# First self attention of a decoder kernel: negative maximum copied into the score banks ahead of the products, rests and maximum on row halves of the array, heads in four steps

## The reference

```python
N_HEADS = 16; HEAD_DIM = 64; SCALE = HEAD_DIM ** (-0.5)
xq = jnp.einsum('bsh,oh->bso', x, wq)          # x: (4, 1024, 256), wq: (1024, 256)
...                                            # xk and xv in the same way
xq = xq.reshape(bsz, N_HEADS, seqlen, HEAD_DIM)   # a reshape, not a transpose
scores = softmax(jnp.einsum('bhid,bhjd->bhij', xq, xk) * SCALE, axis=-1)
out = jnp.einsum('bhij,bhjd->bhid', scores, xv).reshape(bsz, seqlen, N_HEADS * HEAD_DIM)
x = layernorm(x + jnp.einsum('bso,ho->bsh', out, wo))
```

## Time and profile before

| | |
|---|---|
| median of 3 runs | 2979.84 us (2973.99 to 2980.66) |
| profiled execution, first to last instruction (span) | 2978.0 us |
| busy, share of the span: PE | 2631.8 us, 88% |
| DVE | 1704.5 us, 57% |
| ACT | 1190.8 us, 40% |
| POOL | 1621.4 us, 54% |
| first self attention, last `take_out` (L677) | 1738.0 us from the start |

### The profile page before, as it was taken

The page is one execution under the profiler, slowest core; times in us unless marked ns, Lnnn a source line. Parts: engine busy times, 40 slices in busy tenths (PEclk is TensorE's granted clock), DMA queues, the critical chain, the costliest instruction groups (busy, mean ns, idle before and its releaser), DMA issues. The chain is left out here.

```text
span 2978.0 us, 43667 instructions
## 1 busy us (share of the span) xinstructions
PE 2631.8 (88%) x12081; PEld 1634.0 (55%) x12081; DVE 1704.5 (57%) x3436; ACT 1190.8 (40%) x1678; POOL 1621.4 (54%) x1343
## 2 busy tenths in 40 slices
PE   7999999999999999999999968982795588798695
PEld 5666666666666666666666534441574244454254
DVE  5666666656666666665666635662234555468743
ACT  3444444444444444444444324541222333454234
POOL 3666776767766677676776753424334313333343
PEclk8999999999999999999999979996897599899798
DMA  6565455555446445455544320003993100000232
GB/s 176 113 136 113 105 120 113 123 115 114 109 113 138 108 109 121 109 122 114 118 112 108 76 68 23 2 2 126 343 347 128 41 0 1 30 2 9 61 116 88
DMA packets 407010, 303.20 MB, mean 102 GB/s; under 512 B 293558, under 2 KB 338910, under 8 KB 401790
## 3 DMA queue, kind: packets, MB, share of 16 engines
q1 hardware_dynamic: 390734, 231.17, 33.1%
q0 software_dynamic: 12224, 64.71, 6.1%
q10 hardware_dynamic: 3952, 6.08, 0.6%
HBM read 187.04 MB, written 94.39 MB: 95 GB/s over the span
## 5 line engine op out<-in xcount | busy, mean ns | idle before, releaser
L655 POOL TENSOR_TENSOR a_total<-a_total,a_pr 128x1024 f32<-128x1024 f32 x384 | 914.8, 2382 | 46.1 <-ACT a_pr L639 23.4
L639 ACT ACTIVATE a_pr<-a_psS 128x1024 f32<-128x1024 f32 x512 | 525.3, 1027 | 657.3 <-PE a_psS L627 657.3
L584 DVE TENSOR_REDUCE a_nmax<-a_psX 128x1 f32<-128x512 f32 x1024 | 694.2, 687 | 139.9 <-PE a_psX L579 137.8
L667 PE MATMUL a_psO<-a_pr,a_vd 128*64 128x512 f32 x2048 | 481.8, 602 | 0.0
L579 PE MATMUL a_psX<-a_kA,a_qA 128*128 128x512 f32 x1024 | 415.8, 408 | 17.3 <-issue 6.2
L655 POOL TENSOR_TENSOR a_total<-a_pr 128x1024 f32<-128x1024 f32 x64 | 153.3, 2396 | 487.9 <-ACT a_pr L639 487.9
L627 PE MATMUL a_psS<-a_qA,a_kA 128*128 128x512 f32 x1024 | 339.1, 412 | 2.5 <-DVE a_nT L600 1.4
L627 PE MATMUL a_psS<-a_qB,a_kB 128*128 128x512 f32 x1024 | 322.1, 396 | 0.0
L667 PEld LDWEIGHTS a_psO<-a_pr,a_vd 128*64 128x64 f32 x2048 | 129.9, 136 | 239.6 <-issue 188.1
L579 PEld LDWEIGHTS a_psX<-a_kA,a_qA 128*128 128x128 f32 x1024 | 193.9, 189 | 102.2 <-DVE a_nmax L584 23.5
L627 PEld LDWEIGHTS a_psS<-a_qA,a_kA 128*128 128x128 f32 x1024 | 181.2, 189 | 121.5 <-issue 90.1
(11 more groups left out here) (400 smaller groups left out, 4517.5 us busy)
## 6 DMA issues: line engine op xcount, KB each, us to landing
a_qA<-a_qhi SPq DMA_DIRECT2D x124, 256.0 KB
a_vd<-a_vg SPq DMA_DIRECT2D x128, 128.0 KB
a_kA<-a_khi SPq DMA_DIRECT2D x62, 256.0 KB
a_kA<-a_klo SPq DMA_DIRECT2D x62, 256.0 KB
a_kB<-a_khi SPq DMA_DIRECT2D x62, 256.0 KB, 5.6
a_qB<-a_qlo SPq DMA_DIRECT2D x62, 256.0 KB, 5.9
a_qhi<-a_ph SPq DMA_DIRECT2D x120, 128.0 KB, 3.2
a_qlo<-a_pl SPq DMA_DIRECT2D x120, 128.0 KB, 2.7
```

The source lines that it names most:

```text
L584: w.eng.tensor_reduce(nmax[:, half, u:u + 1], psX[:, half, :], AX.X, ALU.max, negate=True)\
L639: w.eng.activation(pr[:, n, :], psS[:, half, :, :].rearrange("p a b -> p (a b)"), ACT.Exp, scale=SCALE)\
L655: w.eng.tensor_tensor(total[:, buf, :], first, pr[:, n, :], ALU.add).then_inc(sems["ad"], 1)
L667: last = w.eng.matmul(psO[q * HD:(q + 1) * HD, :], vd[:, b, kc, :], pr[:, n, q * 512:(q + 1) * 512], start=kc == 0, stop=kc == KC - 1)
```

## The change

- The scores are seeded. `largest` still makes the maxima of the next head, but each VectorE reduction is now 1024 wide, and behind each one VectorE multiplies the identity with the negative maximum (`diag`, a tensor_scalar of 128 x 128). `spread` multiplies ones with `diag` into `psX`, so that each partition holds the negative maxima of all 1024 queries. `seed_new` copies that into the four score banks for the next head, `keep_least` into the SBUF tile `least`, and `seed` copies `least` into a bank pair again for each later step: VectorE the pair 0, ScalarE the pair 1. The products then add onto the seed (`start=False`).
- The rest (low q x high k) is 64 rows deep. `qB` holds q low in both halves, `kB` the second 512 keys of k high, and the product of key tile p runs in rows 0 to 63 of the array while that of key tile p + 4 runs in rows 64 to 127. `largest` does the same: keys 0 to 511 in the lower rows, keys 512 to 1023 in the upper, with high parts alone.
- A head has four steps p with key tiles p and p + 4; the tasks of `misc` have new places (`PLACES`, `TASKS`), two of them at `e`, behind `spread`. `build` is split into four parts that are issued over the steps.
- `max_rows`, `masked`, `rowmask` and the memsets of `qB` and `kB` go.

Core of the diff:

```diff
+                if part == 0:
+                    if j == 0:
+                        w.waits(("sg", AHEAD * 2 * 16), ("sh", (PIECES - AHEAD) * 2 * 16),
+                                *((f"so{n}", w.at(f"so{n}")) for n in range(PIECES)))
+                    w.waits(("s", w.at("s")))
+                    load(kA, 0, lower, khi, f"a{b}")
+                    load(kB, HD, lower, khi, f"a{b}")
+                    load(qA, 0, lower, qhi, f"a{b}")
+                    load(qA, HD, lower, qhi, f"a{b}")
...
+                else:
+                    load(qB, 0, whole, qlo, f"b{b}")
+                    load(qB, HD, whole, qlo, f"b{b}")
...
+                w.eng.matmul(psX[:, 0, :], qA[0:HD, b, u * P:(u + 1) * P], kA[0:HD, b, 0:512], start=True, stop=True)
+                w.eng.matmul(psX[:, 1, :], qA[HD:P, b, u * P:(u + 1) * P], kB[HD:P, b, :], start=True, stop=True)\
...
-                w.eng.tensor_reduce(nmax[:, half, u:u + 1], psX[:, half, :], AX.X, ALU.max, negate=True)\
+                w.eng.tensor_reduce(nmax[:, u:u + 1], psX[:, :, :].rearrange("p a k -> p (a k)"), AX.X, ALU.max, negate=True)\
...
+            w.came["0"] = w.came["1"] = ("mxr", w.count["mxr"])
+            if w.on("vector"):
                 w.wait("mxr", w.at("mxr"))
...
-                w.wait("mt", w.at("mt"))
-                w.link(w.eng.tensor_copy(nT[:, 0, :], psX[0:KC, 0, 0:P]), "dv")
-                w.eng.tensor_tensor(nT[:, 1, :], nT[:, 0, :], psX[0:KC, 0, P:2 * P], ALU.min).then_inc(sems["mn"], 1)
...
-                w.wait("mn", w.at("mn"))
-                w.eng.tensor_tensor(qB[0:KC, b, cols].rearrange("p (u q) -> p u q", q=P),
-                                    nT[:, 1, :].unsqueeze(1).to_broadcast([KC, KC // 2, P]),
-                                    rowmask[:, half * (KC // 2):(half + 1) * (KC // 2), :], ALU.mult).then_inc(sems["mb"], 1)
...
+                if u == 0:
+                    w.wait("bc", w.at("bc"))
+                w.eng.tensor_scalar(diag[:, u * P:(u + 1) * P], ident[:, :], nmax[:, u:u + 1], None, ALU.mult).then_inc(sems["dg"], 1)
+            w.inc("dg")
...
+        def spread(w):
...
+            if w.on("tensor"):
+                w.wait("dg", w.at("dg"))
+                room(w, "0", "1")
                 for q in range(2):
...
+                    last = w.eng.matmul(psX[:, q, :], ones[:, :], diag[:, q * 512:(q + 1) * 512], start=True, stop=True)
+                last.then_inc(sems["bc"], 1)
+            w.inc("bc")
...
+        def keep_least(w):
+            if w.on("vector"):
+                w.wait("bc", w.at("bc"))
+                w.wait("sa", w.at("sa", 2))
+                w.eng.tensor_copy(least[:, 0:512], psX[:, 0, :]).then_inc(sems["lv"], 1)
...
+        def seed_new(w):
...
+            if w.on("vector"):
+                w.wait("bc", w.at("bc"))
+                w.wait("e", w.at("e"))
+                for n in range(2):
+                    w.eng.tensor_copy(psS[:, n, 0, :], psX[:, 0, :]).then_inc(sems["sv"], 1)
...
+                    w.eng.activation(psS[:, n, 1, :], psX[:, 1, :], ACT.Copy).then_inc(sems["sa"], 1)
...
+        def seed(w):
...
+                w.wait("e", w.at("e", 1))
+                w.eng.tensor_copy(both(psS[:, 0, :, :]), least[:, :]).then_inc(sems["sv"], 1)
...
+                w.wait("e", w.at("e"))
+                w.eng.activation(both(psS[:, 1, :, :]), least[:, :], ACT.Copy).then_inc(sems["sa"], 1)
...
+            if w.on("tensor"):
+                if p == 0:
+                    w.wait(f"fb{b}", 6 * 16)
+                    w.wait(f"b{b}", w.at(f"b{b}"))
+                for n in range(2):
+                    kc = p + n * KC // 2
+                    if p > 0:
+                        w.wait(("sv", "sa")[n], w.at(("sv", "sa")[n]))
+                    for q in range(2):
+                        if p == 0:
+                            w.wait(("sv", "sa")[q], w.at(("sv", "sa")[q], 1 - n))
+                        w.eng.matmul(psS[:, n, q, :], kA[:, b, kc * P:(kc + 1) * P], qA[:, b, q * 512:(q + 1) * 512],
+                                     start=False, stop=False, skip_group_check=True)
+                for q in range(2):
+                    cols = slice(q * 512, (q + 1) * 512)
+                    low = w.eng.matmul(psS[:, 0, q, :], kA[0:HD, b, p * P:(p + 1) * P], qB[0:HD, b, cols],
+                                       start=False, stop=True, skip_group_check=True)
+                    high = w.eng.matmul(psS[:, 1, q, :], kB[HD:P, b, p * P:(p + 1) * P], qB[HD:P, b, cols],
+                                        start=False, stop=True, skip_group_check=True)
+                low.then_inc(sems["s"], 1)
+                high.then_inc(sems["s"], 1)
...
+                for p in range(KC // 2):
+                    scores(w, p, b)
+                    if more:
+                        largest(w, 2 * p, nb, start)
+                    for i in (2 * p, 2 * p + 1):
+                        exponent(w, i)
+                        add_up(w, i, j % 2)
+                    if p < 3:
+                        ask(p + 1, 1)
+                        seed(w)
...
-                        piece("1")
+                        ask(0, 2)
+                    if p == 0:
+                        pieces(j, 0)
...
+                    if p == 2 and not start:
+                        turn_back(w)
+                        divide(w, (j - 1) % GH)
...
+                    if p > 0:
+                        values(w, p - 1, b, not (last and j >= GH - 1))
+                    if p == 1 and not start:
+                        misc(w, ("S",), G, (j + 1) % 2)
+                    if more:
+                        largest(w, 2 * p + 1, nb, start)
...
+                        pieces(j, p)
+                values(w, KC // 2 - 1, b)
                 take_out(w)
+                if not (last and j >= 2):
+                    build_v(w, (j + 2) % GH, b)
...
+                    spread(w)
+                    seed_new(w)
+                    keep_least(w)
+                pieces(j, "e")
...
```

More of the change, by code:

```diff
@@ L30, in __init__ @@
         self.mute = False
+        self.came = {}
     def inc(self, name, n=1):
@@ L50, in loop @@
         self.count = dict(start)
+        came = {k: (n, v - per[n]) for k, (n, v) in self.came.items()}
+        self.came = dict(came)
         with eng.Fori(0, trips) as reg:
@@ L55, in loop @@
         self.count = {k: start.get(k, 0) + trips * n for k, n in per.items()}
+        self.came = {k: (n, v + trips * per[n]) for k, (n, v) in came.items()}
 class Writer(Tally):
@@ L420, in misc @@
                     _, tt, c2 = what
-                    w.wait("wl", 3)
+                    if not out:
+                        w.wait("wl", 3)
                     w.wait("xl", w.at("xl"))
@@ L678, in take_out @@
             w.inc("nm")
+            w.came["O"] = ("nm", w.count["nm"])
         def turn_back(w):
@@ L706, in group @@
                 b, nb = j % 2, (j + 1) % 2
-                old = not (first and j == 0)
-                def step(i):
-                    if not more:
-                        return
-                    before = (j - 1) % GH
-                    back = None
-                    if (i == 0 and (before, "3c") in SLOTS) or (i == 1 and (before, "3c") not in SLOTS):
-                        later = [SLOTS[before, where][0] for where in ("3d", "3e") if (before, where) in SLOTS]
-                        back = sum(t in "QKO" for t in later) if not (first and j == 1) else 0
-                    elif i == 1 and (before, "3e") in SLOTS:
-                        back = 0
-                    if i == 13 and (j, "2b") in SLOTS:
-                        back = 0
-                    largest(w, i, nb, back)
```

354 lines of the change are left out of this document (164 added, 190 removed).

## The result

The changed kernel takes 3348.69 us (median of 4 runs, 3346.88 to 3352.80) against 2976.91 us of the kernel before on the same chip: ratio 1.1259, interval 1.1244 to 1.1274. It is slower, as forecast, by 372 us where 230 were forecast; the time lies 9 us above the range. The sign was right, and so was the mechanism named for it, a VectorE instruction held by GpSimd; the loss is 1.6 times the forecast one.

The account below looks back on a forecast made before the run. TensorE's own work was taken to set the pace: 25.0 us plus 5.2 us of waits for VectorE make 30.2 a head against 26.66. With +212 for 60 heads and +19 for the last four, 3210 us; range 3040 to 3340.

Parts of the forecast that it names:

- rival C: In the loop: TensorE's waits let its clock fall, 1.7 us more a head, +109 us, 3320 us; chance 0.14.
- the likeliest case: Whole kernel: the main forecast of 3210 us, with 1 us either way in a head's waits, 3145 to 3275 us; chance 0.47.
- The chain of one step: Per head: TensorE waits on VectorE's maxima, tensor_scalar and seeds, 1.1, 0.4 + 1.5, 0.6 + 1.55 us over steps 1 to 3; together 5.2 us.
- Rival A: In each step: the tensor_scalar does not wait for GpSimd, a head takes 25.6 us, 2913 us in all; chance 0.13.
- The hold: VectorE's tensor_scalar making `diag` waits until GpSimd's addition ends: 1 us in the mean, single ones up to 2.6 us.
- E: VectorE's seeds copied into PSUM are held by GpSimd too, 460 us on top, 3670 us; chance 0.02.
- TensorE's own work: Per head: row-half pairs take one slot each, spread and shape changes add time; from 26.66 to 25.0 us.
- rival D: TensorE's products on row halves do not overlap: +3.8 us of work, a head of 32.0 us, about 3325 us; chance 0.04.
- VectorE's work: Per head: maxima, tensor_scalars, seeds, copies and remaining tasks come to some 21.8 us, less than TensorE's 25.0.
- The sum: Whole kernel: 60 heads at 30.2 instead of 26.66 us, +212; last four heads +19; span 3209 us, time 3210 us.
- Rival B: In the loop: only about half the waits reach TensorE, a head takes 27.9 us, +80, 3060 us; chance 0.18.
- Queues: Loads in `build`: ten issues instead of six and 8% more bytes, costed at 0 in a head of 30.2 us.

Follow-up runs that it names:

- e12: Changed kernel plus six products of 512 columns with a zero weight tile in each step 1, where TensorE waits before the projection: 3317.59 us, ratio 1.1171.
- e10: Changed kernel, plain tensor_scalar kept, with the sum S of step 1 moved ahead of VectorE's seed and the values, moments behind the second maxima: 3281.39 us, ratio 1.1037.
- e1: Changed kernel with the tensor_scalar that makes `diag` also writing an accumulator column nobody reads: 2978.14 us, ratio 1.0022.
- e9: Changed kernel with the accumulator tensor_scalar and the sum S of step 1 ahead of VectorE's seed and the values, moments behind the second maxima: 2942.74 us, ratio 0.9884.
- e2: Changed kernel with GpSimd's softmax-sum additions cut from 1024 columns to 32, tensor_scalar left plain: 2965.57 us, ratio 0.9977.
- e11: Changed kernel with S early and the diagonal written by ScalarE instead of VectorE, but only 291 of 512 diagonals made: 2914.77 us, ratio 0.9802.
- e5: Kernel before the change plus eight plain tensor_scalars a head on VectorE into an unused tile: 3199.37 us, ratio 1.0779.
- e6: Kernel before the change plus eight accumulator-form tensor_scalars a head on VectorE into an unused tile: 3064.67 us, ratio 1.0320.
- e8: Changed kernel with the accumulator tensor_scalar and the four rests of a step issued low, low, high, high: 2978.10 us, ratio 1.0033.

## Why the prediction was right in its sign and wrong in its size

- **The clock was put at nothing: the step that failed, and the largest term of the miss.** The sum has no term for it; it stood as rival C, with 0.14. In the trace the lower clock takes 1.2 us of a head, 74 us in 60 heads, which alone would have taken the time above the likeliest case; without it the time would have been inside the range. When part of it was taken away, 0.46 us of a head came back (e12). The reason given against C, that the new waits are shorter than the 1.84 us of the earlier trace rows and spread out, does not hold. One wait of 2.7 us was not foreseen, but the clock fell behind stops of the foreseen length (1.5 us) too: of the 14 stretches at half in e12 and the 22 in e10, 21 follow a stop of 1.5 us and the other 15 one of 1.9 us. C's price, 1.7 us for each fall, was right; the falls come 27 times in 37 heads. A clock under 1.0 inside the loop was the prediction's own sign of being wrong, and it came.
- **The chain of one step: its list of waits failed, its sum nearly held.** For step 1 the list had "5.36 - 4.27 = 1.1" and looked only at the score products, the maxima and `spread`. It left out that the projection of step 1 writes `psM`, and that the bank is freed by VectorE's transpose behind the held tensor_scalar, the seed and the moments. In the trace step 1 costs 2.2 us (2.73 in the longest). In all TensorE is idle for 210.45 of 1200 us, 5.7 us of a head, where 5.2 were forecast. That the sum is off by only 0.5 us is partly luck: the missed 1.1 us are half made up by waits that came out shorter, 0.4 before the maxima where 1.0 was forecast and 1.3 before the score products behind step 2 where 1.5 was; before `spread` it is 1.7 for 1.55. Rival A's 25.6 us had the same hole, since the wait is there without the hold too (29.5 us in 45 heads of e1, 0.7 us each, and 0.7 us is what the early S gives back in e9).
- **The hold: right, in kind and size.** Forecast mean 1 us and up to 2.6; measured 1054 ns and up to 2.4. Forecast were 4.6 us of a head more idle time of TensorE with it than without; e1 against the kernel after gives 4.5. With the clock that follows, taking the hold away gives 5.9 us of a head (e1, e2). Rival A, that there is no hold, is out. So is E: the seeds take 1214 to 1229 ns each, and no longer than in e2, where there is next to nothing to hold them.
- **What bounds the kernel, and TensorE's own work: right.** A pair on row halves takes one slot (344.46 to 344.80 with its change of shape; the second pair 0.23), so rival D is out. Forecast 25.0 us; in e11, where it is nearly all that is left, 25.07, in e1 25.4. The terms of this sum were not measured one by one.
- **VectorE's work: right.** Forecast 21.8. In e2, with the plain form and no hold, it is 938.90 / 1200 x 26.50 = 20.7; in e1, with the longer accumulator form, 21.2.
- **The sum.** 32.48 - 30.2 = 2.3 us of a head: 0.5 from waits, 1.2 from the clock, and about 0.5 is TensorE's busy time beyond 25.0. Some 0.4 of that is there in e1 at the full clock; it is argued, not shown, that these are the tails of the records before each stop. Times 60 the 2.3 us are 137; the last four heads (30.0 instead of 29 us) add 4, and the part behind the last head took 5 us less than before (1235 against 1240 us). That makes 3345 of the 3209 forecast for the span, as measured.
- **Rival B**, that half the waits would be absorbed, is out in this order. It is what happens in the old one (e5 against e6: 1.8 us of a head).
- **Queues at 0: right.** Waits for loads in front of the maxima are not among the main waits.

Not tried is each part of the change alone (seeding in the old eight steps, or row halves without seeding). So how the 1.3 us between TensorE's 26.4 busy us of a head before and the 25.07 of e11 are shared between row halves, fewer steps and the seeds stays open. Open too is what a whole version of e11 would take.

## What to carry to other kernels

A short VectorE copy or tensor_scalar within SBUF beside long GpSimd instructions should be priced at the end of GpSimd's instruction, and everything that stands behind it in VectorE's queue moves with it. So for a new wait, list every bank and tile that each later instruction of that queue frees, not only what the changed code waits for. If the sum shows TensorE stopping for as long as here, 1.4 to 2.7 us, the lower clock behind the stops belongs in the forecast and not among the rivals; the runs whose longest stop was 0.9 us (e1, e2, e9) kept the full clock in the loop. In a table of waits, read TensorE's loss from the rows of its products and not from those of its weight loads. And count the instructions of a variant against those of its model before its time is believed: e11 was fast with 221 of them missing. Here the idea itself was sound: with the accumulator form and the transpose of S brought forward (e9) it is 1.2% faster than the kernel before.

## What the runs showed of the hardware that I had not expected

- Products on the two row halves start pairwise even where the code issues both products of one half first (e8: 344.21 and 344.55, two starts each). Whether the array or the compiler brings them into this order, the trace does not show. The order within four such products made no difference: 2978.10 against 2978.14 us.
- More work made TensorE faster: six idle-filling products a head, 1.4 us, and the kernel takes 31 us less, because the clock fell less often (14 times against 27 in 1200 us, 0.98 against 0.96).
- The clock was at half for 3.4 us behind stops of 1.4 to 1.9 us too (11 of the 27 times in the kernel after, all 22 in e10), though not behind every such stop.
- The accumulator form of the tensor_scalar, 346 + 83 ns, is cheaper than the plain one with its 285 ns as soon as GpSimd is busy: 370 us of this kernel.
- In a kernel whose TensorE is 99% busy, 3.4 us of extra VectorE work a head were not free, although VectorE was idle for 38% of the time: 1.9 us a head (e6).
